# Score products of an attention kernel over 72 and 74 rows, without zero-filled ones

## The reference

```
x = x + 0.5 * ffn(layernorm(x))     # silu(x wg) * (x wu), 2 of 4 kept, times wd
x = x + attention(layernorm(x))     # 32 heads of 8, 8 key/value heads, rotary, causal
x = x + 0.5 * ffn(layernorm(x))
```

## Time and profile before

| | |
|---|---|
| median of 3 runs | 865.48 us (864.37 to 865.94) |
| the profiled execution | 865.29 us |
| its span, first to last instruction | 863.5 us |
| PE busy | 793.1 us, 92% |
| DVE busy | 736.6 us, 85% |
| ACT busy | 489.4 us, 57% |
| POOL busy | 271.5 us, 31% |
| mean granted PE clock | 0.978 of full |

### The profile page before, as it was taken

One profiled execution on the slowest core, in us unless ns is written; L12 is line 12 of the kernel. 1 busy time (PEld: TensorE's weight loads), 2 busy tenths in 40 slices (PEclk: granted clock), 3 DMA queues, 4 the chain that ended last, 5 costly groups with the idle time before them and its releaser, 6 DMA issues.

```text
span 863.5 us, 15657 instructions
## 1 busy us (share of the span) xinstructions
PE 793.1 (92%) x5119; PEld 468.6 (54%) x5168; DVE 736.6 (85%) x1896; ACT 489.4 (57%) x953; POOL 271.5 (31%) x339
## 2 busy tenths in 40 slices
PE   4899999797779999999999999999999899999986
PEld 3678887675623333343333333333333358888876
DVE  3989999957699889888898898988998159999996
ACT  6444344212326777777778777777777744443441
POOL 1154433346621212322121221255314210533250
PEclk9999999898879999999999999999999999999998
DMA  8100000045932212332123311632123000000001
GB/s 282 51 0 2 1 1 0 1 128 161 283 86 74 61 22 73 89 77 53 30 76 77 76 47 33 173 80 72 31 60 92 14 12 1 1 25 1 25 1 49
DMA packets 32769, 52.30 MB, mean 61 GB/s; under 512 B 3664, under 2 KB 19920, under 8 KB 31536
## 3 DMA queue, kind: packets, MB, share of 16 engines
q1 hardware_dynamic: 32624, 51.23, 21.7%
q10 hardware_dynamic: 64, 0.07, 0.0%
HBM read 20.94 MB, written 15.47 MB: 42 GB/s over the span
## 4 chain that ended last, share of the span: by engine, by line
PE 55%; DVE 8%; ACT 5%; issue 3%; PEld 1%; PEldq 0%; another core or an unknown queue 0%; DVEq 0%; ACTq 0%
PE att_o_ps L1342 15%; PE att_m_ps L1312 14%; PE att_s_ps L1326 13%; ACT att_probs L1449 4%; PE ffn_gate L218 4%; PE ffn_up L218 3%; PE ffn_y_ps L356 3%; PEld ffn_y_ps L356 1%; DVE att_scratch L1399 1%; DVE ffn_hs L495 1%; DVE att_maxima L1402 1%; PE out_y_ps L1112 1%; DVE ffn_h L513 1%; DVE ffn_pair_min L474 1%; DVE ffn_pair_max L473 1%
## 5 line engine op out<-in xcount | busy, mean ns | idle before, releaser
L1449 ACT ACTIVATE att_probs<-att_s_ps 128x512 f32<-128x512 f32 (+1 forms) x640 | 308.0, 555 | 112.9 <-PE att_s_ps L1326 96.6
L1399 DVE CUSTOM_DVE_ANT_0 att_scratch<-att_m_ps,att_causal 128x512 bf16<-128x512 f32 (+3 forms) x512 | 234.1, 485 | 27.5 <-PE att_m_ps L1312 24.7
L1312 PE MATMUL att_m_ps<-mk,mq 128*128 128x384 bf16 (+3 forms) x736 | 229.4, 333 | 17.9 <-DVE att_maxima L1399 11.1
L1326 PE MATMUL att_s_ps<-sq,sk 128*128 128x512 bf16 (+3 forms) x751 | 212.4, 328 | 7.0 <-ACT att_probs L1449 3.7
L1402 DVE TENSOR_REDUCE att_maxima<-att_m_ps 128x1 f32<-128x512 f32 x256 | 175.7, 687 | 11.8 <-PE att_m_ps L1312 10.3
L1342 PE MATMUL att_o_ps<-att_probs,att_vs 128*32 128x512 f32 (+3 forms) x1536 | 157.0, 496 | 0.2
L1502 POOL TENSOR_SCALAR_AFFINE_SELECT att_probs<-att_probs 128x512 f32<-128x512 f32 x128 | 79.0, 635 | 237.3 <-ACT att_probs L1449 237.3
L1312 PEld LDWEIGHTS att_m_ps<-mk,mq 128*128 128x128 bf16 x768 | 72.8, 98 | 116.5 <-DVE att_maxima L1399 53.8
L1326 PEld LDWEIGHTS att_s_ps<-sq,sk 128*128 128x128 bf16 x768 | 71.3, 98 | 112.5 <-ACT att_probs L1449 74.6
L578 POOL TENSOR_TENSOR ffn_hs_lo<-ffn_hs,ffn_hs_hi 128x512 fp32r<-128x512 f32 x56 | 91.0, 1649 | 126.0 <-ACT ffn_hs_hi L410 126.0
L432 ACT ACTIVATE ffn_a<-ffn_h 128x512 f32<-128x512 f32 x64 | 40.5, 633 | 106.9 <-DVE ffn_h L513 106.9
(11 more groups left out here) (112 smaller groups left out, 1178.5 us busy)
## 6 DMA issues: line engine op xcount, KB each, us to landing
q_rows<-qkv_parts SPq DMA_DIRECT2D x24, 384.0 KB, 4.0
mq<-q_rows SPq DMA_DIRECT2D x16, 576.0 KB
sq<-mq SPq DMA_DIRECT2D x16, 576.0 KB
k_rows<-qkv_parts SPq DMA_DIRECT2D x12, 192.0 KB, 3.0
mk<-k_rows SPq DMA_DIRECT2D x16, 144.0 KB
sk<-mk SPq DMA_DIRECT2D x16, 144.0 KB
sq<-att_shift_t SPq DMA_DIRECT2D x128, 2.0 KB
out_num<-att_sums SPq DMA_DIRECT2D x128, 16.0 KB
```

The lines of the kernel that those rows point to most:

```text
L1312: pe.matmul(m_ps[bank][:, :n], mq[g % 2][:, h, t * P:(t + 1) * P], mk[g % 2][:, kc * N:kc * N + n], start=True, stop=True).then_inc(m_done, 1)
L1326: last = pe.matmul(s_ps[(u * QPK + h) % S_BANKS][:, at:at + w], sk[g % 2][:, kb * P:(kb + 1) * P], sq[g % 2][:, h, qc * N + q0:qc * N + q0 ...
L1399: dve.tensor_tensor_reduce(out=scratch[bank][:, :n], in0=m_ps[bank][:, :n], in1=causal[:, N - n:], scale=1.0, scalar=LOWEST, op0=ALU.add, ...
L1449: act.activation(probs[u % len(probs)][:, h, SPAN[u]], s_ps[(u * QPK + h) % S_BANKS][:, SPAN[u]], ACT.Exp, scale=SCALE).then_inc(exp_done, 1)
```

## The change

The products read only the first 72 rows (`m`) or 74 rows (`s`) of their operands. With that nothing reads the other rows, so the zero fills of `mq`, `mk` and `sq` are taken out, and with them SP's wait ahead of `load_m`. `sk` is still set to -1 in all rows, since its rows 72 and 73 are read. The entries of `between` move up: the causal mask (`before_groups`) now stands in the first gap, the fill of `sk0` in the second and that of `sk1` in the third; POOL's program of attention starts with the zero of `vs`.

```diff
@@ sync of the Q/K/V phase
         for g in range(2):
-            sp.wait_ge(group_rows.filled, 2 * g + 2)
             group_rows.load_m(sp, g)
@@ GroupRows
-    def fill_m(self, pool, e):
-        self.zero(pool, (self.mq[e], self.mk[e]))
-
     def fill_s(self, pool, e):
-        self.zero(pool, (self.sq[e],))
         pool.memset(self.sk[e][:], -1.0).then_inc(self.filled, 1)
-
-    def zero(self, pool, tiles):
-        for tile in tiles:
-            flat = tile[:].rearrange("p h t -> p (h t)") if len(tile.shape) == 3 else tile[:]
-            pool.memset(flat.bitcast(F32), 0.0).then_inc(self.filled, 1)
...
         if g < 2:
-            sp.wait_ge(self.filled, 6 + 2 * g)
+            sp.wait_ge(self.filled, g + 1)
@@ tensor of attention, m_item and s_head
-                pe.matmul(m_ps[bank][:, :n], mq[g % 2][:, h, t * P:(t + 1) * P], mk[g % 2][:, kc * N:kc * N + n],
+                pe.matmul(m_ps[bank][:, :n], mq[g % 2][:ROWS, h, t * P:(t + 1) * P], mk[g % 2][:ROWS, kc * N:kc * N + n],
...
-                last = pe.matmul(s_ps[(u * QPK + h) % S_BANKS][:, at:at + w], sk[g % 2][:, kb * P:(kb + 1) * P],
-                                 sq[g % 2][:, h, qc * N + q0:qc * N + q0 + w], start=True, stop=True)
+                last = pe.matmul(s_ps[(u * QPK + h) % S_BANKS][:, at:at + w], sk[g % 2][:ROWS + SHIFT, kb * P:(kb + 1) * P],
+                                 sq[g % 2][:ROWS + SHIFT, h, qc * N + q0:qc * N + q0 + w], start=True, stop=True)
@@ gpsimd of attention
-        group_rows.fill_s(pool, 1)
         for e in range(2):
             pool.memset(vs[e][:], 0.0).then_inc(ones_ready, 1)
@@ build
-        between += [lambda pool: group_rows.fill_m(pool, 0),
-                    lambda pool: (before_groups(pool), group_rows.fill_m(pool, 1)),
-                    lambda pool: group_rows.fill_s(pool, 0)]
+        between += [before_groups, lambda pool: group_rows.fill_s(pool, 0), lambda pool: group_rows.fill_s(pool, 1)]
```

## The result

The change made the kernel slower: 869.06 us (median of 5 executions, 867.91 up) against 864.51 (863.65 to 865.94), a ratio of 1.0046 with a 95% interval of 1.003 to 1.0062. One of the five took 890.64 us, with a mean clock of 0.937; it is outside the comparison. The forecast was 859.2 us, faster, and its range ended at 867.

What follows compares the result with a forecast made beforehand. Chunks were taken as bound by a cross-engine chain, the lead-in by DVE, groups by PE. From 865.29 us, 5.24 for three gaps and 0.85 for the clock came off, products 0: 859.2 us, range 856 to 867.

Steps and rivals of the forecast that it cites:

- What bounds the kernel: Whole kernel: a chain across engines bounds the Q/K/V chunks, DVE the attention lead-in, PE the steady groups.
- DVE sets the pace: Attention lead-in, 232 to 262: DVE busy 28.62 of 30 us, PE 19.34, so a slower PE clock is covered.
- The three gaps: Between Q/K/V chunks: fewer POOL fills shorten DVE's waits by 1.32, 2.21 and 1.71 us, 5.24 in all.
- The bonus for the clock: Behind the first two chunk gaps: shorter PE pauses may hold the clock; bounds 0 and 2.7 us, 0.85 taken.
- The products, "I take 0": m and s products in 16 groups: contracting over 72 or 74 rows instead of 128 changes their time by 0.
- the first rival: Lead-in and groups: few rows count less for PE's clock; 24.5 us per half-clock group, up to 1250 us total; chance 0.15.
- Might never get back: First rival, steady groups: a gap-free 72-row stream starting at the lower clock might stay there; all 16 groups cost 392 us.
- Value steps keep their full rows: Groups, argument against the first rival: value steps don't change and are a third of the work.
- the granted clock follows pauses wherever I see it fall: Profile before, argument against the first rival: clock drops go with pauses in PE's work.
- Loads, stores: Two rivals: weight loads double without 128 rows (890 us, chance 0.04); chunk stores keep the gaps long (864.5 us, 0.12).

Runs made afterwards that it cites:

- rows74: act_fills with both m and s products over 74 rows; median 867.23 us, ratio 1.002.
- rows_only: The kernel before with only the row slices cut (m 72, s 74), all POOL fills kept; 873.17 us, ratio 1.0105.
- act_fills: The changed kernel with products over 128 rows again and the zero fills done by ACT; 860.61 us, ratio 0.9954.
- rows88: act_fills with both m and s products over 88 rows; median 863.68 us, ratio 0.9984.
- rows80: act_fills with both m and s products over 80 rows; median 867.41 us, ratio 1.0027.
- heat_pause: The changed kernel plus unused 128-row products ahead of and among group 0's m products, and five in the pause before group 1's; 867.42 us, ratio 1.0028.
- m80_s96: act_fills with m products over 80 rows and s products over 96; median 867.36 us, ratio 1.0019.
- warm_pause: act_fills plus five unused products of 128 rows by 512 columns ahead of group 1's first m product; 859.71 us, ratio 0.9947.

## Why the prediction was wrong

**What bounds the kernel.** Right for the chunks and the groups. "DVE sets the pace" in the lead-in held only at the clock that it then had. With the clock low to its end, PE's work there is 26.73 of 30 us, from 254 on PE is full, and the stretch behind it is PE's.

**The three gaps.** Forecast 1.32, 2.21 and 1.71 us, 5.24 in all, and 0.85 for the clock: 6.09. Measured 5.67, of which 0.27 was there before the first gap, at 180 us. The waits fell by 0.93, 1.79 and 1.31 (1.84 to 0.91, 2.70 to 0.91, 3.12 to 1.81), each 0.39 to 0.42 less than forecast. In the first two gaps POOL's L173 took 0.65 and 0.61 us in place of the 0.23 of the earlier trace rows; in the third `turned` took 1.69 in place of 1.29. The remaining 1.4 us (5.67 - 0.27 - 4.03) are other shortenings of the same chain. The bonus for the clock must be among them. Behind the first gap the clock fell all the same (0.50 from 196.8 to 200.2; before, from 197.6 to 201.0); behind the second it was 0.70 on average in 215 to 220 before and 1.00 in 210 to 225 after. PE's own gaps shrank to 2.68 and 2.16 us, forecast 2.2 and 1.8. How much of the 1.4 us is the clock wasn't measured apart. This step held.

**The products, "I take 0".** This term was wrong twice. At one clock it is nearly 0: 512 columns have their 0.22 us with 72 rows as with 128. The Trainium skill ("TensorE: Matmul & The Clock Gate", "Why this matters for your kernels") says the same of 32 rows, and the trace agrees for 72. But the switch between 72 and 74 rows costs about 2 ns behind a product of 512 columns, 1.38 us from the fifth to the last split; only the switch, since rows74 takes it away. That alone would not have spoiled the forecast.

**The step that failed** is the one behind the first rival: "If they count less, the lead-in stays at the lower clock for longer, which DVE covers. It decides from the point where a steady group starts at the lower clock." With it the sum of the forecast put the slower clock of the products at nothing. Rows do count (rows_only, act_fills, and the series 128, 96, 88, 80, 74 with its return at 258, 264, 272, 276, 276). DVE covered the lower clock only until about 254. From there PE was full: 1.97 us were lost between the second and third split, and 4.43 more between the third and fourth, where the first half of group 0 (262 to 275) ran at half clock. Together they make up nearly all of the +6.41 us between the first maxima and the fifth split; rows74 against act_fills gives 6.25 for the rows alone, rows_only 8.88 against before. The rival had this mechanism, with a chance of 0.15 and a price of 24.5 us for each whole group; it took the condition to be rarer than it was, and its price, counted in whole groups, was too high. The 5.67 us gained ahead of attention and the 6.41 lost behind it nearly cancel, so the small difference of the totals says little about either. "Might never get back" was right for a stream of 72-row products, as far as the 6 us at 241.56 show, but in every run the clock was back before the fifth split. What brought it back wasn't taken apart. "Value steps keep their full rows" was named against the rival, and they may have bounded its price: the return comes just behind one in the changed kernel and rows_only. In rows88 (272.3) it comes 0.6 us ahead of one and 2.6 us behind the end of the one before.

The argument against it, "the granted clock follows pauses wherever I see it fall", was no evidence. The score products of that trace all had 128 rows, so their rows could not vary. The padding, which does nothing for the result, kept up the clock: 56 (`m`) and 54 (`s`) of the 128 rows in the kernel before and in act_fills. Products without it cost 0.9% to 1.05% here (the change against act_fills, 1.0046 to 0.9954, and rows_only, 1.0105), and most of that by the clock, not by the products' own time. The Trainium skill's "Always tile to 128 partitions" ("Trainium Kernel Development and Optimization", "Best Practices") names no price; the tiles kept their 128 partitions in every run here, and only what the products read was cut.

**Loads, stores.** Both rivals fell: loads stayed at 97 ns, and no gap kept its length. The argument against the first, that every row shows a load paced by columns, was not in the rows: both loads of the earlier trace rows have 128 columns.

**Open.** The last stretch, from the last split to the end, is 0.58 us longer after the change, and between 193.2 and 194.8 us over all kernels; no experiment looked at it. Why single executions of rows80, rows74, heat_pause and m80_s96 are shorter, with a higher mean clock (862.22, 859.08, 862.42 and twice 863.29 us), isn't known; they weren't profiled.

## What to carry to other kernels

Before rows are cut from a product because they are zeros, ask whether the stage has pauses that drop TensorE's clock: the zero rows cost the product no time, and they may be what brings the clock back. Here it paid to keep the padding and to move the fills to an engine that had time (act_fills, 860.61 us). An engine that is "covered" at its present clock has to be costed at the other one, up to the first stretch in which it is the bound.

## What the runs showed of the hardware

- The granted clock answers to the rows over which products contract. Without pauses, 13 products of 72 or of 74 rows in 6.01 us stayed at the lower clock, and within 10 of 128 rows in 4.06 us at the same place the higher one came back; 72 and 74 rows lost the clock at 257.5 where 128 kept it (heat_pause, warm_pause). The answer is graded between 80 and 96 rows (median 867.4, 863.7 and 861.4 us at 80, 88 and 96; 860.6 at 128). Rows of zeros count for it (rows74 against act_fills).
- `m` and `s` products with different row counts stand about 2 ns further apart than ones with equal counts: 1.35 to 1.4 us from the fifth to the last split, 13.5 groups. Beside the value steps, which have 128 rows, no such cost shows (372.29 us with 74 rows, 372.30 with 128).
- A tiny POOL operation (L173, 128x4) took 0.23 us where two fills, one of them 128x2048, stood ahead of it, 0.65 behind the mask and 0.61 behind the fill of `sk0` alone. The `turned` behind the fills of the third gap went the same way, from 1.29 to 1.69. No run shows why.
